# Keys, values and the running state of a causal linear attention turned, multiplied and kept as float16 halves

## What is computed

```python
x1 = x + attention(layernorm(x))
# attention: q, k = relu(.) + 1e-6 and v, from one projection of 512 to 1536
#   kv[l] = sum over l' <= l of k[l'] v[l']^T ; den[l] = q[l] . sum over l' <= l of k[l']
#   out[l] = (q[l] . kv[l]) / max(den[l], 1e-6), then a projection 512 to 512
out = x1 + int8_linear(layernorm(x1))   # one scale over all tokens
```

## Time and profile before

| | |
|---|---|
| median of three runs | 1286.04 us |
| the profiled execution, its span | 1286.96 us, 1285.2 us |
| TensorE matmuls busy | 89% of the span |
| VectorE, GpSimd, ScalarE busy | 83%, 55%, 43% |
| mean granted TensorE clock | 0.967 of 2.4 GHz |
| first stage, to about | 1162 us |

### The profile page before, as it was taken

One profiled execution on the slowest core, in us unless ns is written; L12 is line 12 of the kernel. 1 busy time (PEld: TensorE's weight loads), 2 busy tenths in 40 slices (PEclk: granted clock), 3 DMA queues, 4 the chain that ended last, 5 costly groups with the idle time before them and its releaser, 6 DMA issues. The chain is left out here.

```text
span 1285.2 us, 31799 instructions
## 1 busy us (share of the span) xinstructions
PE 1148.5 (89%) x10931; PEld 848.0 (66%) x10931; DVE 1071.6 (83%) x2431; ACT 550.9 (43%) x1130; POOL 701.5 (55%) x847
## 2 busy tenths in 40 slices
PE   4699999999899989999899989999999999974998
PEld 2477677777667766776677666776776777742664
DVE  5678889888798888888788979888888898767887
ACT  4344444444344433444444444443444444422553
POOL 2355556555555555555455555555555565540887
PEclk8889999999899999999899989999999999987999
DMA  5122223222222232322222222232232231240994
GB/s 212 50 59 75 78 75 86 77 75 76 67 78 75 79 85 75 83 78 76 69 79 75 74 70 78 80 83 77 82 82 68 79 86 43 52 156 17 336 343 172
DMA packets 73933, 120.92 MB, mean 94 GB/s; under 512 B 16433, under 2 KB 16945, under 8 KB 73778
## 3 DMA queue, kind: packets, MB, share of 16 engines
q1 hardware_dynamic: 72528, 117.51, 30.9%
q10 hardware_dynamic: 1250, 1.32, 0.3%
HBM read 36.97 MB, written 31.46 MB: 53 GB/s over the span
## 5 line engine op out<-in xcount | busy, mean ns | idle before, releaser
L396 POOL TENSOR_SCALAR_AFFINE_SELECT am_hi<-am_hi 128x512 f16<-128x512 f16 x256 | 174.4, 681 | 389.1 <-DVE am_lo L854 389.1
L446 PE MATMUL unit<-xt_hi,w_hi 128*128 128x256 f16 x1024 | 286.9, 280 | 20.5 <-DVE xt_lo L830 10.9
L446 PE MATMUL unit<-xt_lo,w_hi 128*128 128x256 f16 x1024 | 286.5, 280 | 0.0
L446 PE MATMUL unit<-xt_hi,w_lo 128*128 128x256 f16 x1024 | 286.1, 279 | 0.0
L374 POOL TENSOR_SCALAR q_t<-q_t,eps_scaled 128x256 f32<-128x256 f32 x128 | 119.3, 932 | 132.7 <-ACT q_t L658 132.7
L396 POOL TENSOR_SCALAR_AFFINE_SELECT am_lo<-am_lo 128x512 f16<-128x512 f16 x256 | 178.9, 699 | 0.0
L854 DVE SCALAR_TENSOR_TENSOR am_lo<-sc,am_hi 128x512 f16<-128x512 f32 x256 | 163.5, 679 | 16.1 <-ACT am_hi L685 15.9
L658 ACT ACTIVATE q_t<-unit,qk_bias_scaled 128x256 f32<-128x256 f32 x128 | 60.8, 475 | 227.4 <-PE unit L446 227.4
L685 ACT ACTIVATE am_hi<-sc 128x512 f16<-128x512 f32 x256 | 138.6, 596 | 41.4 <-PE sc L478 41.4
L446 PEld LDWEIGHTS unit<-xt_hi,w_hi 128*128 128x128 f16 x1024 | 102.9, 101 | 46.9 <-DVE xt_lo L830 17.5
L917 DVE TENSOR_TENSOR state<-st,state 32x66 f32<-32x66 f32 x384 | 85.1, 222 | 48.1 <-PE st L550 43.5
(11 more groups left out here) (150 smaller groups left out, 2798.9 us busy)
## 6 DMA issues: line engine op xcount, KB each, us to landing
stack<-qk_hi SPq DMA_DIRECT2D x512, 64.0 KB, 2.0
xs<-x SPq DMA_DIRECT2D x64, 256.0 KB, 2.6
stack<-qk_lo SPq DMA_DIRECT2D x256, 64.0 KB, 2.0
out<-res SPq DMA_DIRECT2D x64, 256.0 KB, 3.6
x_spill<-xs SPq DMA_DIRECT2D x56, 256.0 KB, 2.1
x_ring<-x_spill SPq DMA_DIRECT2D x56, 256.0 KB, 4.1
stack<-qkv_wt SPq DMA_DIRECT2D x4, 768.0 KB, 9.2
stack<-out_wt SPq DMA_DIRECT2D x1, 1024.0 KB, 13.2
```

Source lines behind the costliest of these rows:

```text
L396: ins = pool.affine_select(out=am[:, r, :, :], in_=am[:, r, :, :], compare_op=ALU.is_ge, fill=0.0, base=0, pattern=[[0, HG], [1, CHUNK]], ...
L446: mm = pe.matmul(dst[:, 0:GT], wp[:, k, f:f + P], xp[:, g % 2, k, :], start=(n == 0), stop=(n == len(terms) - 1))
```

## The change

- Epsilon is no longer added by GpSimd. ScalarE adds it in qk_hi and VectorE in qk_lo, for keys and queries alike. One buffer f_t takes the place of q_t and k_t; qk_hi and qk_lo are kept for two groups.
- Keys are turned as float16 (hi and lo, eight transposes with a float16 identity) into a bank of `unit`, directly after the attention result, and copied by one ScalarE instruction (`copy_keys`). The table of banks gets an entry ("kt") after "xt", so each unit behind it in the chunk moves to the other bank.
- Keys times values is three float16 matmuls for each of the four blocks, and so is queries times state.
- Keys times values moves ahead of, and behind, the output projection; the additions to the state move ahead of, and behind, `residual`. An addition is one instruction on all 128 partitions and 264 elements, the blocks that nobody reads included.
- New: `split_state`, in the next chunk after `split_attn`: four instructions on ScalarE (s_hi) and four on VectorE (s_lo), each 32 partitions and 132 elements.
- Scales of v, of the ones column and of the division are changed so that the halves keep in range.

```diff
-            UNITS = [[("xt", 0)] + [("qk", i) for i in range(2, QK)],
-                     [("xt", 1), ("v", 0), ("v", 1), ("qk", 0), ("qk", 1)]]
+            UNITS = [[("xt", 0), ("kt", 0)] + [("qk", i) for i in range(2, QK)],
+                     [("xt", 1), ("kt", 1), ("v", 0), ("v", 1), ("qk", 0), ("qk", 1)]]
...
+                        elif was == "kt":
+                            pe.wait_ge(kn_done, upto_inner(b, wc))
...
+                def transpose_keys(b, c):
...
+                    dst = take_bank(b, "kt", c, 0).bitcast(F16)
+                    for p, part in enumerate((qk_hi, qk_lo)):
+                        for g in range(HG):
+                            mm = pe.transpose(dst[:, (p * HG + g) * P:(p * HG + g + 1) * P], part[:, par, g, at], ident_half[:, :])
+                    mm.then_inc(kt_ready, 1)
...
-                        pe.wait_ge(s_updated, upto_inner(b, c - 1, 2, half + 1))
+                        pe.wait_ge(s_lo_done, upto_inner(b, c - 1))
...
+                            for qp, sp_ in ((qk_hi, s_hi), (qk_hi, s_lo), (qk_lo, s_hi)):
+                                pe.matmul(o[:, half, i * 4 * VW:(i + 1) * 4 * VW], qp[:, par, HG + g, at],
...
-                        pe.wait_ge(s_updated, upto_inner(b, c, 2, half))
+                        pe.wait_ge(s_added, upto_inner(b, c, 2, half))
+                    terms = ((0, v_hi), (0, v_lo), (1, v_hi))
...
                         if not (first and c == 0):
                             transpose_attn(b, c - 1)
+                        if c < CB - 1:
+                            transpose_keys(b, c)
                         projections(2 if c % GROUP == 0 else 1)
                         scores(b, c, 2, first)
                         scores(b, c, 3, first)
                         if c % GROUP == 1:
                             projections(1)
+                        if c < CB - 1:
+                            keys_values(b, c, 0, first)
                         if not (first and c == 0):
                             project_out(b, c - 1)
+                        if c < CB - 1:
+                            keys_values(b, c, 1, first)
                         projections(1)
-                        if c < CB - 1:
-                            transpose_keys(b, c, first)
                         outputs(b, c, 0, first)
                         if c % GROUP == 0:
                             projections(1)
                         outputs(b, c, 1, first)
-                        if c < CB - 1:
-                            keys_values(b, c, 0, first)
                         projections(len(todo))
-                        if c < CB - 1:
-                            keys_values(b, c, 1, first)
...
+                def copy_keys(b, c):
+
+                    act.wait_ge(kt_ready, upto_inner(b, c))
+                    act.activation(kn[:, :, :, :], unit[:, unit_bank[("kt", c % GROUP)], :].bitcast(F16).rearrange(
...
+                def split_state(b, c):
+
+                    act.wait_ge(s_added, upto_inner(b, c, 2))
...
+                    for r in range(4):
+                        own = (slice(D * r, D * (r + 1)), slice(None), r, slice(None))
+                        ins = act.activation(s_hi[own], state[own], ACT.Copy)
+                    ins.then_inc(s_hi_done, 1)
...
+                    own = state[:, 2 * half:2 * half + 2, :, :].rearrange("p g h w -> p (g h w)")
+                    new = st[:, 0:8 * VW]
...
+                        ins = dve.scalar_tensor_tensor(out=own, in0=new, scalar=SCORE_FACTOR, in1=own, op0=ALU.mult, op1=ALU.add)
+                    ins.then_inc(s_added, 1)
+
+                def split_state(b, c):
+
+                    dve.wait_ge(s_hi_done, upto_inner(b, c))
                     for r in range(4):
...
+                        own = (slice(D * r, D * (r + 1)), slice(None), r, slice(None))
+                        ins = dve.tensor_tensor(s_lo[own], state[own], s_hi[own], ALU.subtract)
+                    ins.then_inc(s_lo_done, 1)
```

More of the change, by code:

```diff
@@ L212, in build @@
             am_lo = buf(one, "am_lo", [P, 4, HG, CHUNK], F16)
-            qk_hi = buf(one, "qk_hi", [P, QK, GT], F16)
-            qk_lo = buf(one, "qk_lo", [P, QK, GT], F16)
+            qk_hi = buf(one, "qk_hi", [P, 2, QK, GT], F16)
+            qk_lo = buf(one, "qk_lo", [P, 2, QK, GT], F16)
+            kn = buf(one, "kn", [P, 2, HG, P], F16)
             stack = buf(one, "stack", [P, 2, 2, HEADS, GT], F16)
@@ L247, in build @@
             v_bias_scaled = buf(one, "v_bias_scaled", [P, E])
-            kn = buf(one, "kn", [P, HG, P])
             state = buf(one, "state", [P, HG, 4, VW])
+            s_hi = buf(one, "s_hi", [P, HG, 4, VW], F16)
+            s_lo = buf(one, "s_lo", [P, HG, 4, VW], F16)
             den = buf(one, "den", [P, 2, HB])
@@ L276, in projections_of @@
             def projections_of(c, last):
-                units = [(c // GROUP + (2 if u in UNITS[1] and u[0] == "qk" else 1), u) for u in UNITS[c % GROUP][1:]]
+                units = [(c // GROUP + (2 if u in UNITS[1] and u[0] == "qk" else 1), u) for u in UNITS[c % GROUP][2:]]
                 return [(g, u) for g, u in units if not (last and g >= CB // GROUP)]
@@ L484, in transpose_attn @@
                     pe.wait_ge(attn_ready, upto(b, c, 2))
-                    if c % CB < CB - 1:
-                        pe.wait_ge(kn_copied, upto_inner(b, c))
+                    if not (isinstance(b, int) and b * CB + c == 0):
+                        pe.wait_ge(x1_ready, upto(b, c - 1))
                     for i in range(EC):
@@ L499, in project_out @@
                     mm.then_inc(op_ready, 1)
-                def transpose_keys(b, c, first):
-                    par, at = place(c)
-                    if not (first and c == 0):
-                        pe.wait_ge(x1_ready, upto(b, c - 1))
-                    for g in range(HG):
-                        mm = pe.transpose(misc[:, g * P:(g + 1) * P], k_t[:, par, g, at], ident[:, :])
-                    mm.then_inc(kn_ready, 1)
                 def outputs(b, c, half, first):
@@ L521, in outputs @@
                     if c > 0:
-                        pe.wait_ge(s_updated, upto_inner(b, c - 1, 2, half + 1))
+                        pe.wait_ge(s_lo_done, upto_inner(b, c - 1))
                         for i in range(2):
                             g = 2 * half + i
-                            pe.matmul(o[:, half, i * 4 * VW:(i + 1) * 4 * VW], q_t[:, par, g, at],
-                                      state[:, g, :, :].rearrange("p h w -> p (h w)"),
-                                      start=clear, stop=False, skip_group_check=True)
-                            clear = False
+                            for qp, sp_ in ((qk_hi, s_hi), (qk_hi, s_lo), (qk_lo, s_hi)):
+                                pe.matmul(o[:, half, i * 4 * VW:(i + 1) * 4 * VW], qp[:, par, HG + g, at],
+                                          sp_[:, g, :, :].rearrange("p h w -> p (h w)"),
+                                          start=clear, stop=False, skip_group_check=True)
+                                clear = False
                     for n in range(HB):
```

148 lines of the change are left out of this document (75 added, 73 removed).

## The result

The changed kernel takes 1290.36 us (median of 13 runs, 1287.84 to 1293.94), the kernel before 1286.95 us in the same comparison (13 runs, 1284.56 to 1290.68): ratio 1.0027, 95% interval 1.0018 to 1.0037. It is slower by 3.4 us, just over what can be told from no change. The forecast was 1288 us, 2 us slower.

What follows compares the result with a forecast made beforehand. A loop was taken to bound: VectorE through the odd chunk up to xt_lo, then TensorE to the even chunk's end. From 1286.0 us, 11 - 1 - 2 - 6 = +2 gave 1288 us, 8-in-10 range 1262 to 1314.

Steps and rivals of the forecast that it cites:

- +11, -1, -2, -6: Forecast change in us: middle pairs +11, pairs across batch ends -1, ahead of batch 0 -2, last batch -6; sum +2.
- What bounds the kernel: Odd-even chunk pair, 34.42 us: VectorE through the odd chunk to xt_lo, 20.7, then TensorE to the even chunk's end, 13.6.
- The odd chunk: From odd chunk's start: am_lo 2 ends 2.0 us later, late additions gone save 1.9, xt_lo at 20.8 us, +0.1.
- The hand-over: Odd chunk, ScalarE's s_hi to VectorE's s_lo: s_hi done at 5.15 us, VectorE idle from 4.42 to 5.2.
- The even chunk: After xt_lo: +1.31 waiting before qk 2, -0.42, -0.44 and -0.37 saved, +0.4 for the first addition; sum +0.5 us.
- 6.0: +0.4: Even chunk: first addition done 6.4 us after xt_lo, TensorE at the second state product after 6.0, so it waits 0.4.
- Both shrink, -2: Ahead of batch 0: VectorE's 2.04 us wait for queries and 3.65 us of four qk_lo shrink, -2 us.
- I put them at -0.1 each: Pairs of chunks across a batch's end, with no state on one side and stalls of their own: -1 us in all.
- The last batch: TensorE's 2.18 us wait for am_lo and a half-clock output projection's 2.6 us go: -6 us, bounds -3 and -9.
- What would show it: Signs: pair 34.4 to 35.2 us, even-chunk xt_lo wait 1.5 to 2, VectorE idle before s_lo, last batch 4 us shorter.
- the rivals: Hand-over short, 1262 us (chance 0.22); hand-over long, 1314 us (0.20); TensorE's clock falls once a pair, 1328 us (0.08).
- The long hand-over: Every s_lo meets a GpSimd mask, 3.0 us for four, s_hi at 5.75: +1.7 us a pair, 1314 us; chance 0.20.

Runs made afterwards that it cites:

- The two doublings: Changed kernel with every float16 state product done twice, either in odd chunks 1, 3, 5 (1293.84 us) or in even chunks 0, 2, 4, 6 (1313.39 us).
- the additions in blocks: Changed kernel with each state addition again as four instructions of 32 partitions instead of one of 128 x 264: 1312.84 us, ratio 1.0208 to the kernel before.
- the early split: Changed kernel with the state left by an even chunk split into halves at that chunk's end, in second buffers: 1246.55 us, ratio 0.969 to the kernel before.
- s_hi first: Changed kernel with ScalarE's four s_hi moved ahead of its copy of the turned keys: 1288.41 us, ratio 1.0011 to the kernel before.
- the keys later: Changed kernel, even chunks only: keys turned after projections qk 2 and qk 3, first state product behind the output projection: 1291.08 us.
- the epsilon alone: Kernel before with only the queries' epsilon moved from GpSimd's additions into ScalarE's and VectorE's splits: 1284.05 us, ratio 0.998.

## Why the prediction was right

The sign and the size were right, but the sum owes part of that to errors that cancel: +11, -1, -2, -6 were forecast, and +4.0, -0.7, +1.2, -3.5 came. And a forecast of +2 lay inside the 2.6 us that it said a measurement can tell, so the sign was in part luck. By its own steps:

**What bounds the kernel.** The loop of VectorE through the odd chunk and TensorE after xt_lo held: 20.79 + 13.75 us are the pair of 34.60, within 0.06. The two doublings, the additions in blocks and the early split moved it in the direction that it gives, the early split by half of the size in the pair. The two misses (s_hi first, the keys later) show what it leaves out: the masks of GpSimd, which lengthen VectorE's steps and end about when TensorE needs them.

**TensorE's work.** Three float16 products in place of one in float32 leave TensorE 268 instead of 276 us of work in 300, and the pair did not feel it in odd chunks.

**The odd chunk.** at_lo ends 4.47 us after the start (forecast 4.42), s_hi 5.46 (5.15; bounds 4.9 and 5.75), VectorE is idle 1.02 (0.8), the instruction behind am_lo 2 starts at 8.9 (8.8), xt_lo ends at 20.79 (20.8). The hand-over is dearer than forecast by 0.3 because the four s_hi of 0.31 us stand 0.32 apart, not 0.2; the s_lo took 1.37 instead of 1.65 us, since the late s_hi let the masks pass, and were done at 6.9 (6.8). The loss and the gain cancel, as forecast: am_lo 2 ends 2.1 us later than before (8.97 against 6.84 after the chunk's start; forecast 2.0), and from there to the end of xt_lo it takes 2.1 us less (11.82 against 13.89; forecast 1.9 less).

**The even chunk.** The time from xt_lo to the chunk's end was forecast to rise by 0.5 us and rose by 0.12 (13.63 to 13.75). The term that was mis-sized is the wait for the addition, "6.0: +0.4". The first addition is done 6.1 us after xt_lo (662.80 + 0.42 - 657.08; forecast 6.4, the four s_lo took 1.98 us and not 2.2), and TensorE comes 6.1 us after it (forecast 6.0): the second product, at 663.28, waits 0.1. The wait for xt_lo is 1.47 us as said. So 0.3 of the 0.4 us did not come; over 22 pairs that is some 7 us of the sum.

**Ahead of batch 0.** "Both shrink, -2" was wrong in its mechanism. VectorE's wait for the queries hardly shrank (2.04 us before, 2.14 with the epsilon alone, 1.85 now). Its four qk_lo did, from 3.73 to 1.68 us, but TensorE starts the values almost where it did: at 48.89 with the epsilon alone, 49.02 before. The 2.7 us of that run are a matter of the clock. Before, TensorE waits 3.67 us ahead of the values and is granted 0.50 of 2.4 GHz (half clock) from 49 to 52 us; with the epsilon alone it waits 1.79 us and is granted 1.00. The 12 matmuls of v 0 take 5.28 us in the one and 2.75 in the other. The kernel before, then the epsilon alone:

```profile
49.00:52.00 3.00, 2.98 (x8) 1.08 (x9) 0.47 (x1) 0.00 (x0) 0.00 (x0) 0.50 0.44 109
49.02 0.59 PE L454 MATMUL unit<-w_hi,xt_hi 128*128 128x512 f16 x1 [3.67 <-DVE xt_lo L830]
```

```profile
49.00:52.00 3.00, 3.00 (x15) 1.36 (x14) 0.60 (x2) 1.39 (x1) 0.00 (x0) 1.00 0.40 100
48.89 0.38 PE L451 MATMUL unit<-w_hi,xt_hi 128*128 128x512 f16 x1 [1.79 <-DVE xt_lo L828]
```

The first residual of the changed kernel starts 3.9 us later than that of the run with the epsilon alone, which was not in the sum. The new table of banks puts both turned x into bank 0, and the second waits for xt_lo of the first:

```profile
44.43 0.60 PE L432 MATMUL unit<-ident,xn 128*128 128x128 f32 x4
47.95 0.82 PE L432 MATMUL unit<-ident,xn 128*128 128x128 f32 x4 [2.92 <-DVE xt_lo L852]
50.28 0.58 PE L464 MATMUL unit<-w_hi,xt_hi 128*128 128x512 f16 x1 [1.50 <-DVE xt_lo L852]
```

In the kernel before, the eight ran together at 44.26. The values begin 1.4 us later than with the epsilon alone, and v 0 runs at half clock again, 5.13 us, which is 2.4 more. That the bank is the cause of both was not tested by a run of its own.

**The pairs across a batch's end.** "I put them at -0.1 each" was a guess without a mechanism. In straight code they lose 2.1 to 2.5 us. Chunk 7 has the hand-over (its four s_lo take 2.02 us) but never had additions of its own to save, and in chunk 0 behind it am_lo 2 waits 0.96 us for ScalarE. At the loop's jump they win 1.0 on average, which nothing in the prediction foresaw: a gap of 1.0 to 1.6 us that TensorE had there is gone, and three of the five batches, those granted more clock, take 139.0 to 139.1 us, while the two at the clock of before take 140.7 (last section). With all five at 140.7 the change would by this estimate have been some 5 us slower; in that much, the forecast was lucky.

**The last batch.** Shorter by 3.5 us, inside the bounds, short of the 6. The half clock did not go away, and a wait of 2.84 us for the masks is new ahead of the last outputs. Before, one output projection of 12 matmuls took 5.26 us (from 1138.02; 2.76 is normal); now one takes 3.60 (from 1138.88) and the last of all 4.25 (from 1161.43): in these projections 2.5 us are lost before and 2.3 after.

**What would show it.** The period lies within 34.4 to 35.2, the wait for xt_lo is 1.5 us, the norm's multiplication still takes 1.11 us; VectorE's idle time before s_lo was 1.0, at the top of its 0.5 to 1. The last batch missed its 4 us by half a microsecond. None of the rivals came. The long hand-over "decides from am_lo 2 later than 9 us", and it was 8.9 to 9.0, close to that mark; but its terms did not come: s_hi at 5.46 and not 5.75, s_lo of 1.37 and 1.98 us and not 3.0, and a pair 0.18 longer and not 1.7.

The profiled executions differ by 0.9 us and the medians by 3.4. The runs of each kernel spread by 6 us; where the other 2.5 us lie is open, since one execution of each has a trace.

## What to carry to other kernels

Split the loop at the instruction that hands over between the two full engines and price each edit on the side that counts there: here 0.69 us of TensorE made the pair 0.46 us longer in one chunk and 0.19 in the other. A gain in a chunk is safe only if the engine that gets it waits for nothing new ahead of it; look first for the place where the same hand-over fits into an idle stretch, which was worth 44 us here, while doing it sooner at the same place was worth 2. When the totals say more than the pairs, look at the clock at the batch ends before giving it to the edit. When a table of buffers or banks gets a new member, follow every one of its users round once more, those ahead of the loop too.

## What the runs showed of the hardware

- TensorE's clock at the start of a batch differs between kernels, and between batches of one. Windows of 14 us from the loop's jump, the third to last column is the granted clock; first the kernel before, the first and the third of the five batches:

```profile
336.00:350.00 14.00, 12.21 (x101) 8.95 (x102) 8.28 (x14) 6.57 (x14) 6.19 (x9) 0.76 0.13 36
...
616.00:630.00 14.00, 11.82 (x86) 8.62 (x87) 8.64 (x15) 6.16 (x14) 5.78 (x9) 0.76 0.12 33
```

The changed kernel at the same batches:

```profile
339.00:353.00 14.00, 11.31 (x126) 9.19 (x127) 10.62 (x19) 6.94 (x14) 6.39 (x9) 1.00 0.17 46
...
617.00:631.00 14.00, 12.32 (x92) 9.36 (x93) 9.01 (x17) 6.70 (x13) 5.64 (x9) 0.76 0.11 32
```

  Before, gaps of 2.69 and 1.57 us on "issue" stand 2.9 us apart, and 24 matmuls of projections take 5.1 us from 339.60, where 2.8 is normal: half clock, 1.2 GHz. The mean is 0.76 in all five. After, the second gap is gone, a wait of 0.6 to 2.3 us for xt_lo stands in its place, and the five are 1.00, 0.88, 0.76, 0.88, 0.76. It is tempting to blame the second gap, but the other runs do not bear that out. The doubled odd products have it in four of the five batches (1.04 to 1.32 us; 1.32 at 487.39) and are granted 1.00 in those four; the additions in blocks do not have it and are at 0.76 in all five batches. One window of each:

```profile
484.00:498.00 14.00, 11.72 (x128) 9.41 (x129) 10.53 (x18) 7.07 (x14) 6.40 (x9) 1.00 0.18 47
```

```profile
345.00:359.00 14.00, 12.01 (x91) 8.88 (x92) 9.20 (x22) 6.57 (x13) 5.66 (x9) 0.76 0.11 32
```

  The doubled even products have the second gap (1.81 to 2.15 us) and 0.76 in all five. What decides the clock there stays open.
- Four ScalarE copies of 32x132, each in another block of partitions, stand 0.32 us apart at a length of 0.31; with 128 partitions and a scale per partition each is 0.43 long, and the four with the step to the next instruction take 1.19 us in place of 1.31.
- The same four VectorE subtractions took 1.18, 1.37, 1.98 and 2.03 us, as GpSimd was at rest, ended its last mask, or had more of them under way (the last two): a wait ahead of such instructions can be half paid for by what it lets pass.
